# Moving router steps, layer norm and a quarter of the grouped scaling in a two-layer transformer kernel

## The reference, cut to what matters

```python
xn = layernorm(x)
x = x + L0_attn(xn) + L0_ffn(xn)
# L0_attn: 16 query heads of 64 over 4 key/value heads, rotary, causal with a decaying bias:
scores = Q @ K.T / 8 + polarity_bias + (1 - gtp) * NEG
out = softmax(scores) @ V @ Wo
# L0_ffn: y = xn + mha(rmsnorm(xn, g1)), 16 heads of 16, rotary, causal; then y + moe(rmsnorm(y, g2)):
probs = softmax(xf @ w_router)           # 8 experts
g, eidx = top_k(probs, 2)                # each expert then takes its 320 best tokens
```

## Time and profile before

| | us |
|---|---|
| median of 3 runs | 4479.95 |
| runs | 4475.49 to 4479.95 |
| profiled execution, own time | 4474.58 |
| its span | 4472.5 |
| TensorE busy | 3949.0 (88%) |
| DVE busy | 2916.6 (65%) |
| GpSimd busy | 2591.0 (58%) |
| ScalarE busy | 2582.7 (58%) |

### The profile page before, as it was taken

One profiled execution on the slowest core, in us unless ns is written; L12 is line 12 of the kernel. 1 busy time (PEld: TensorE's weight loads), 2 busy tenths in 40 slices (PEclk: granted clock), 3 DMA queues, 4 the chain that ended last, 5 costly groups with the idle time before them and its releaser, 6 DMA issues. The chain is left out here.

```text
span 4472.5 us, 105750 instructions
## 1 busy us (share of the span) xinstructions
PE 3949.0 (88%) x37596; PEld 2580.4 (58%) x37596; DVE 2916.6 (65%) x8580; ACT 2582.7 (58%) x6209; POOL 2591.0 (58%) x4110
## 2 busy tenths in 40 slices
PE   2899899999999999999999999829499999999999
PEld 1555555555555555555555556526266666666666
DVE  3665666665666656656666656562377777878786
ACT  2556556566565565565565665502166767777776
POOL 2567577586585675675765865625354545555452
PEclk7999999999999999999999999959799999999999
DMA  4334234243243233342432432123333343434341
GB/s 109 69 74 91 65 93 84 60 103 73 72 89 73 72 86 73 85 91 60 98 77 67 95 75 73 48 92 59 48 52 59 49 62 49 62 50 60 56 54 24
DMA packets 215158, 317.07 MB, mean 71 GB/s; under 512 B 22192, under 2 KB 161776, under 8 KB 212592
## 3 DMA queue, kind: packets, MB, share of 16 engines
q1 hardware_dynamic: 209520, 300.88, 32.8%
q0 software_dynamic: 3968, 5.25, 0.7%
q10 hardware_dynamic: 1152, 4.19, 0.2%
HBM read 126.66 MB, written 32.59 MB: 36 GB/s over the span
## 5 line engine op out<-in xcount | busy, mean ns | idle before, releaser
L1380 POOL TENSOR_SCALAR l_prob_wo<-l_prob_wo,l_recip_g 128x128 f32<-128x128 f32 (+3 forms) x1024 | 1097.8, 1089 | 232.3 <-DVE l_recip_g L966 231.7
L1820 DVE TENSOR_REDUCE l_neg_max<-l_bank 128x1 f32<-128x512 f32 x1024 | 681.0, 684 | 288.0 <-PE l_bank L1659 287.0
L1946 ACT ACTIVATE l_pts<-l_bank 128x512 f32<-128x512 f32 x1024 | 593.4, 597 | 310.1 <-PE l_bank L1674 301.4
L960 DVE CUSTOM_DVE_ANT_0 l_prob_wo<-l_bank,l_bias 128x128 f32<-128x128 f32 (+3 forms) x1024 | 477.1, 485 | 412.4 <-PE l_bank L683 388.5
L1219 ACT ACTIVATE l_prob_wo<-l_prob_wo,l_neg_max_g 128x128 f32<-128x128 f32 (+3 forms) x1024 | 571.0, 559 | 294.4 <-DVE l_neg_max_g L960 291.3
L947 DVE CUSTOM_DVE_ANT_0 l_bank<-l_bank,l_mask 128x128 f32<-128x128 f32 (+3 forms) x1024 | 502.9, 499 | 354.8 <-PE l_bank L632 347.1
L1211 ACT ACTIVATE l_pts<-l_bank 128x128 f32<-128x128 f32 (+3 forms) x1024 | 438.4, 437 | 451.3 <-PE l_bank L650 435.2
L694 PE MATMUL l_bank<-ident,l_prob_wo 128*128 128x128 f32 x2560 | 432.7, 283 | 95.4 <-POOL l_prob_wo L1380 43.4
L694 PEld LDWEIGHTS l_bank<-ident,l_prob_wo 128*128 128x128 f32 x2560 | 287.9, 141 | 335.8 <-POOL l_prob_wo L1380 191.5
L1659 PE MATMUL l_bank<-next_ks,l_qs 96*128 96x512 bf16 x1024 | 394.9, 386 | 60.0 <-DMA next_ks<-l_parts 30.5
L1368 POOL CAST l_max_parts<-l_neg_max 128x4 bf16<-128x4 f32 x256 | 49.9, 195 | 631.1 <-DVE l_neg_max L947 630.8
(11 more groups left out here) (261 smaller groups left out, 8083.7 us busy)
## 6 DMA issues: line engine op xcount, KB each, us to landing
l_bias<-bias SPq DMA_DIRECT2D x128, 512.0 KB, 4.4
l_qs<-l_parts SPq DMA_DIRECT2D x384, 128.0 KB
l_ks<-l_parts SPq DMA_DIRECT2D x192, 128.0 KB
next_ks<-l_parts SPq DMA_DIRECT2D x192, 128.0 KB
l_x<-in_x SPq DMA_DIRECT2D x32, 512.0 KB, 4.6
l_kT<-l_bias SPq DMA_DIRECT2D x128, 128.0 KB, 3.3
l_qT<-l_arena SPq DMA_DIRECT2D x128, 128.0 KB, 3.3
l_qT<-l_bias SPq DMA_DIRECT2D x128, 128.0 KB, 3.0
```

Source lines behind the costliest of these rows:

```text
L960: nc.vector.tensor_tensor_reduce(prob[qt][:, i, :], G4[v % 4][:, 0:w], bias[:, g % 2, i, T - w:T], -1.0 / ROOT, 3.0e38, ALU.add, ALU.min, ...
L1380: nc.gpsimd.tensor_scalar(prob[qt][:, i, :], prob[qt][:, i, :], recip_g[:, k:k + 1], None, ALU.mult).then_inc(s.g_scaled, 1)
L1820: nc.vector.tensor_reduce(neg_max[:, n % (2 * UNITS):n % (2 * UNITS) + 1], S[n % SB][:, :], AX.X, ALU.max, negate=True).then_inc(s.max_rea ...
L1946: nc.scalar.activation(pts[:, q % 2, u % H, :, :], TB[u % 2][:, :].rearrange("p (j q) -> p j q", j=NT), ACT.Exp, scale=DS ** -0.5).then_in ...
```

## The change

- Router: step 0 stays in slot 119; the rest becomes six steps, in slots 24, 26, 32, 37, 41 and 48 of the next frame. The gate transpose moves from slot 20 to 52, its copy from 21 to 53, its store on SP behind the first two bias loads.
- Layer norm of batch c + 1 (not c): statistics in slots 114 to 117, variance in 120, centring in 123 to 126 of frame f, the power on GpSimd in 121. Batch 0 is normed in the first slot of frame -1. The squares move on ScalarE from slots 12 to 15 to slots 2 to 5. The x load moves on SP behind the bias load of group 7, ahead of the store of the normed batch; for batch 1 behind the stacking of batch 0.
- GpSimd: each pair of rotations, rests and lows is spread over two slots, most a slot or two apart.
- Scaling: for pairs with qt 0 and 1, unit i = 1 is scaled on DVE, right behind the pair's reciprocal. That is 16 of 64 per frame.

```diff
+        def scaled_on_pool(p, i):
+            return i == 0 or p % NT > 1
+
+        def scaled(b, p, i):
+            qt = p % NT
+            if scaled_on_pool(p, i):
+                return s.g_scaled, 6 * (PAIRS * b + p // NT) + (1, 2, 3, 5)[qt] + i
+            return s.g_scaled_v, 2 * (PAIRS * b + p // NT) + qt + 1
...
-                    pe.wait_ge(s.g_scaled, v + 1)
+                    pe.wait_ge(*scaled(b, p, i))
...
-                        if r == 20:
+                        if r == 52:
                             fill_gT(f - 1, 1)
...
                     nc.vector.reciprocal(recip_g[:, k:k + 2], sums_g[:, k:k + 2]).then_inc(s.g_recip, 1)
+                    if not scaled_on_pool(p, 1):
+                        dve.wait_ge(s.g_recip, BEATS * b + p + 1)
+                        v = prob[p % NT][:, 1, :]
+                        nc.vector.tensor_scalar(v, v, recip_g[:, k + 1:k + 2], None, ALU.mult).then_inc(s.g_scaled_v, 1)
...
-                        if r == 21:
+                        if r in (24, 26, 32, 37, 41, 48):
+                            router(f - 1, 1 + (24, 26, 32, 37, 41, 48).index(r))
+                        if r == 53:
                             copy_gT(f - 1)
...
-                        if r in (119, 122, 124, 126):
-                            router(f, (119, 122, 124, 126).index(r))
+                        if r == 119:
+                            router(f, 0)
                     if there(c):
-                        if 2 <= r < 6:
-                            statistics(c, r - 2)
-                        if r == 7:
-                            variance(c)
-                        if 10 <= r < 14:
-                            centre(c, r - 10)
...
+                    if c == 0 and r == 0:
+                        for t in range(NT):
+                            statistics(0, t)
+                        variance(0)
+                        for t in range(NT):
+                            centre(0, t)
+                    if there(c + 1):
+                        if 114 <= r < 118:
+                            statistics(c + 1, r - 114)
+                        if r == 120:
+                            variance(c + 1)
+                        if 123 <= r < 127:
+                            centre(c + 1, r - 123)
                     if n == -1:
                         make_bias()
...
-                        if 12 <= r < 16:
-                            squares(c, r - 12)
+                        if 2 <= r < 6:
+                            squares(c, r - 2)
...
                         if r >= 68:
-                            scale(f, (r - 68) // 2, r % 2)
-                        if r in (7, 12, 17):
-                            rotate_g(f, (r - 7) // 5)
+                            if scaled_on_pool((r - 68) // 2, r % 2):
+                                scale(f, (r - 68) // 2, r % 2)
+                        if r in (6, 8, 12, 13, 17, 18):
+                            rotate_g(f, (6, 8, 12, 13, 17, 18).index(r) // 2, (6, 8, 12, 13, 17, 18).index(r) % 2)
...
-                        if r == 87:
-                            rotate_g(f, 4)
+                        if r in (87, 89):
+                            rotate_g(f, 4, (r - 87) // 2)
...
-                        if r == 68:
-                            rotate(c, 1)
-                        if r == 73:
-                            rest(c, 1)
-                        if r == 78:
-                            low(c, 1)
+                        if r in (66, 67):
+                            rotate(c, 1, r - 66)
+                        if r in (73, 74):
+                            rest(c, 1, r - 73)
+                        if r in (78, 80):
+                            low(c, 1, (r - 78) // 2)
...
+                sp.dma_start(x[:, :, :], a["x"][0]).then_inc(s.x_loaded, 16)
                 for f in range(-1, B + 1):
                     c = f + 1
-                    if there(c):
-                        wait(sp, s.xp_ready, 2 * f)
-                        if f > 0:
-                            sp.wait_ge(s.xp_ready, 2 * f)
-                        sp.dma_start(x[:, :, :], a["x"][c]).then_inc(s.x_loaded, 16)
...
                     if there(f):
                         load_bias(f, 7)
+                    if there(f) and there(c + 1):
+                        sp.wait_ge(s.xp_ready, 2 * (f + 1))
+                        sp.dma_start(x[:, :, :], a["x"][c + 1]).then_inc(s.x_loaded, 16)
+                    if f == -1:
+                        sp.wait_ge(s.ln, LN_STEPS)
+                        sp.dma_start(x[:, :, :], a["x"][1]).then_inc(s.x_loaded, 16)
+                    if there(f):
                         sp.wait_ge(s.xf_ready, NT * (f + 1))
```

More of the change, by code:

```diff
@@ L539, in layer0 @@
             sem(n) for n in ("scores_ready", "max_ready", "split", "max_turned", "max_placed", "t_ready", "exp_ready", "pv_ready", "out_turned"))
-        s.g_scores, s.g_max, s.g_exp, s.g_recip, s.g_scaled, s.g_turned, s.g_copied_v, s.g_copied_a, s.g_pv, s.g_out = (
-            sem("g_" + n) for n in ("scores", "max", "exp", "recip", "scaled", "turned", "copied_v", "copied_a", "pv", "out"))
+        s.g_scores, s.g_max, s.g_exp, s.g_recip, s.g_scaled, s.g_scaled_v, s.g_turned, s.g_copied_v, s.g_copied_a, s.g_pv, s.g_out = (
+            sem("g_" + n) for n in ("scores", "max", "exp", "recip", "scaled", "scaled_v", "turned", "copied_v", "copied_a", "pv", "out"))
         s.w_ready = sem("w_ready")
@@ L1087, in router @@
                         link(nc.vector.tensor_tensor(pr[:, :, :], pr[:, :, :], scalars[:, 1, :].unsqueeze(2).to_broadcast([P, NT, E]), ALU.mult))
+                    if step == 2:
                         for t in range(NT):
@@ L1090, in router @@
                         link(m)
-                    if step == 2:
+                    if step == 3:
                         for t in range(NT):
@@ L1095, in router @@
                         link(nc.vector.tensor_copy(top_f[:, :, :], top_i[:, :, :]))
+                    if step == 4:
                         for t in range(NT):
@@ L1098, in router @@
                         link(m)
-                    if step == 3:
+                    if step == 5:
                         for t in range(NT):
@@ L1102, in router @@
                         link(m)
+                    if step == 6:
                         link(nc.vector.tensor_tensor(one_hot[:, :, :], pr[:, :, :], lg[:, :, :], ALU.mult))
@@ L1380, in scale, with rotate_g @@
                     nc.gpsimd.tensor_scalar(prob[qt][:, i, :], prob[qt][:, i, :], recip_g[:, k:k + 1], None, ALU.mult).then_inc(s.g_scaled, 1)
-                def rotate_g(b, m):
+                def rotate_g(b, m, half):
                     w = work[(1, 0, 1, 1, 0)[m]]
@@ L1385, in rotate_g, with rotate, rest, low @@
                         pool.wait_ge(*W.emptied(("rope", b, m, e)))
[L1386 to L1389 removed]
+                    nc.gpsimd.tensor_tensor(w[:, half, :], w[:, half, :], w[:, 2 + half, :], (ALU.subtract, ALU.add)[half]).then_inc(s.turned_g, 1)
+                def rotate(c, a2, half):
                     for e in range(2):
                         pool.wait_ge(*W.emptied(("qk", c, 2 * a2 + e)))
[L1392 to L1403 removed]
+                    nc.gpsimd.tensor_tensor(arena[:, half, :], arena[:, half, :], arena[:, 2 + half, :], (ALU.subtract, ALU.add)[half]).then_inc(s.rot_ready, 1)
+                def rest(c, a2, e):
+                    pool.wait_ge(s.high_done, 4 * c + 2 * a2 + e + 1)
+                    nc.gpsimd.tensor_tensor(arena[:, 2 + e, :], arena[:, e, :], parts[2 * a2 + e][:, 0, :], ALU.subtract).then_inc(s.rest_ready, 1)
+                def low(c, a2, e):
+                    pool.wait_ge(s.mid_done, 4 * c + 2 * a2 + e + 1)
+                    nc.gpsimd.tensor_tensor(parts[2 * a2 + e][:, 2, :], arena[:, 2 + e, :], parts[2 * a2 + e][:, 1, :], ALU.subtract).then_inc(s.low_done, 1)
                 def scale_out(b, g):
@@ L1423, in _ @@
                     c = f + 1
+                    if c == 0 and r == 0:
+                        power(0)
+                    if there(c + 1) and r == 121:
+                        power(c + 1)
                     if there(f):
@@ L1452, in _ @@
                             nc.gpsimd.tensor_tensor(rms[:, :], mean_sq[:, :], minus_half[:, :], ALU.pow).then_inc(s.pow_rms, 1)
[L1453 to L1464 removed]
+                        if r in (40, 41):
+                            rotate(c, 0, r - 40)
+                        if r in (49, 50):
+                            rest(c, 0, r - 49)
+                        if r in (54, 56):
+                            low(c, 0, (r - 54) // 2)
+                        if r in (66, 67):
[4 more added lines that the diff above has]
+                            low(c, 1, (r - 78) // 2)
             @block.sync
@@ L1517, in _ @@
                         sp.dma_start(x[:, :, :], a["x"][f]).then_inc(s.x_again, 16)
-                    if there(f - 1):
```

(2 more changed lines are left out.)

39 lines of the change are left out of this document (11 added, 28 removed).

## The result

The changed kernel takes 4452.9 us in the median (4451.8 to 4455.8, 5 runs) against 4479.95 for the kernel before (4475.5 to 4485.5, 5 runs): ratio 0.994, interval 0.9925 to 0.9954. It is faster by 27 us. The forecast was 4498, slower; the time lies at the very end of its range, and the sign is wrong.

What follows compares the result with a forecast made beforehand. TensorE, busy 88% of the span, was taken as the bound. Frame terms -24.0 (15 frames) and +30.1 (14 frames), plus +17.4 at the start, gave +23.5 on 4474.6: 4498 us, range 4452 to 4535.

Steps and rivals of the forecast that it cites:

- Start: Start of layer 0: bias tables and first row maximum wait for batch 1's x load and layer norm, +17.4 us.
- The x load: Slot 114: DVE stalls 3.2 us for the next batch's x, making TensorE late by 1.8 us per frame.
- Router in slots 24 to 48: nothing: The router's six pieces hide in DVE's waits for scores there: no cost, or 0.5 us per frame if uncovered.
- -0.15: Slot 124: the router's 1.4 us leaves, but centring and a scaling take its place, -0.15 us per frame.
- Last slots otherwise, +0.35: Last slots besides the x wait: variance in slot 120 +0.5, router's leaving -0.15, together +0.35 us per frame.
- DVE's share of the scaling, +1.0: Grouped half: DVE's scalings delay five of eight copies for transposes by 0.2 us each, +1.0 us per frame.
- GpSimd, -1.2: Grouped half: sixteen scalings leave GpSimd and TensorE's waits on it shrink, -1.2 us per frame.
- the 0.68 us at 1259.78: A TensorE wait on GpSimd, to vanish with half a pair and a scaling less before it.
- Small-head half, -1.4: Slot 17: GpSimd's earlier first rotation lets key halves land sooner, shortening TensorE's wait by 1.4 us per frame.
- Faster: Rival: all 2.65 us of waits on GpSimd go, x stall hidden, DVE's scaling costs 0.2; 4439 us, chance 0.16.
- third rival: Slower by much: DVE's scalings wait out GpSimd's running one, 48 us more, 4546 us; chance 0.08.

Runs made afterwards that it cites:

- Experiment 2: The changed kernel with the x load of the next batch issued on SP ahead of the bias load of group 7: 4420.7 us, ratio 0.9876.
- Experiment 11: The changed kernel with GpSimd's pairs in one piece again: 4493.1 us, ratio 1.0016 to the kernel before.

## Why the prediction was wrong

The sum was 23.5, the profiles differ by -20.7: 44 us. Of these frames 0 to 14 hold 33, frame 15 and the experts' stage 8.5, chance in layer 1 7.4, and the start -4.6 (it was worse than I said). By part, with the ratios above times 4480:

| part | booked in the prediction | put in alone | put back |
|---|---|---|---|
| layer norm's move | +17.4 + 25.2 + 7.0 and a share of -21 | +89 | -66 |
| router's move | 0, and a share of -0.15 x 14 | -48 | +42 |
| pairs spread | -18 and a share of -21 | -22 | +34 |
| quarter on DVE | +15 | -25 | +15 |

Put in alone, the four make -6, together -27: the parts help each other, and the layer norm's move most, at +89 alone and +66 beside the others. The clock is a large part of that: alone, the move adds eight frames with a lowered clock in slots 17 to 21 (1.7 us each) and seven in the last slots (1.0 each), and in the changed kernel there is none in either place. By these counts that is an estimated 20 of the 23 us; against the second profile of the kernel before, which has four and nine such frames, it is 15.

- **Start: right in mechanism, sized low.** 22.0 us against 17.4. x landed at 95.2, not 90.5; the layer norm (4.45) and the tables (29.6) took what the sum said.
- **The x load: right.** The wait is 3.9 us (46.4/12) instead of 3.2, and TensorE's loss 1.9 against 1.8. Experiment 2 shows it.
- **"Router in slots 24 to 48: nothing" and "-0.15": the step that failed by most.** That the pieces are hidden in their new place was right. What they cost in the old one was not asked. I had the row with 1.57 us on the table, and let the centring take the router's place, which kept the wait in the sum. The router's leaving is worth 2.5 to 2.8 us per frame, some 0.5 of it by the clock that is not lowered behind the wait.
- **"Last slots otherwise, +0.35": right only as a net sum.** It hides -2.5 for the router and +2.4 for the layer norm, which I had at +0.5 for the variance alone; GpSimd's power behind that variance, ahead of four scalings, was left out. Where only one of the two happens, the net no longer holds: in frames 14 and 15 no next batch is normed, so the router's share, the small-head half's 2.0 and the grouped half's 1.1 stand uncompensated. They make 5.6 us, and frame 15 was in fact 5.8 us shorter up to its last store, but frame 14 only 3.1, with 3.4 us more at the lower clock in its middle. Single frames differ by up to 2.5 us between two profiles of one kernel, so the match in frame 15 is partly luck. The sum counted 15 frames at -1.6 and left the sixteenth out.
- **"DVE's share of the scaling, +1.0" beside "GpSimd, -1.2": the sum of the two is what the steady frame had most wrong.** Five of the eight copies were to be late by 0.2 us; in the changed kernel TensorE is late for them in two slots, by 0.2 and 0.4, as much of the scaling falls in DVE's wait for the transpose ahead of the copy, which the earlier trace rows showed at 0.33 us. The relief of GpSimd outweighs that: the 0.68 us at 1259.78 went, as forecast, and came back as 0.79 when the scalings did. Together the grouped half gained 1.1 per frame, not 0.2.
- **The net of a steady frame.** It was missed by 0.9 us in the grouped half, 0.6 in the small-head half and 0.55 in the last slots, where the router's error of 2.4 hides behind the layer norm's of 1.9. Over 14 or 15 frames these make some 30 of the 33 us, so the router's term alone does not explain the wrong sign.
- **Small-head half, -1.4: right in mechanism, sized low.** 2.0 us. Experiment 11 puts the wait back into slot 17 (0.51 to 2.04 us) with the pairs, which fits the chain through GpSimd's first rotation that the prediction named; that rotation alone was not tested. The layer norm's leaving brings little without the split rotations: 0.4 us alone, and the lowered clock behind the longer wait turns it into a loss of 0.8.
- **The rivals.** "Faster" gave 4439 by another way, with GpSimd's waits gone and x in time. Neither came: the stall stood at 3.9 us and the waits on GpSimd fell by a tenth. The result had the sign of this rival and not its mechanism.
- **The 4546 of the third rival** did not come, but DVE scalings that wait out an operation of GpSimd exist; see below.

What stays open: why the wait in slot 17 is longer with the layer norm gone and the pairs whole (2.0 us and more) than in the kernel before (1.4 to 2.1) was not traced DMA by DMA, nor why the same wait lowers the clock in one frame and not in the next.

## What to carry to other kernels

When a step is moved, price its old place as carefully as its new one: find the wait of the bound engine behind it, and ask what is gone if it goes. Two moves into and out of the same slots must be priced one by one, not as a net sum, because frames at the edges and later edits see only one of them. Put parts of a change on the chip one by one, each alone and each taken out: here three of four parts gain and the fourth costs 62 us, and the whole hides it. And count a wait of the bound engine together with the clock of the work behind it, which can change from frame to frame at the same wait.

## What the hardware showed

**The clock behind a wait.** Waits of 1.57 and 0.25 us in a busy stretch were followed by 3.4 us at 1.2 GHz in seven of 14 frames of the kernel before, and 16 products then took 3.1 to 3.25 instead of 1.74 us; the other seven frames had the same waits and kept 2.4 GHz. Behind 0.44 us of waiting (router alone) or 0.86 (the changed kernel) in that slot the clock never fell. In all these kernels the longer wait in slot 63 (31.5 us in 13 frames, 2.4 each) has 3.4 to 6.8 us at the lower clock around or behind it in every one of frames 1 to 14. And the dips in the last slots go with the wait there: none in 14 frames in the kernels with the router moved and the wait in slot 126 below 1 us, seven to fourteen where it is 1.57 us and more. No experiment here removes the wait in slot 63.

**GpSimd and DVE.** In the changed kernel a scaling on DVE that starts while GpSimd runs one of its operations of two inputs with 256 or 512 elements per partition lasts until that one has ended: 45 of 45 such cases, ending 83 to 150 ns after it in the mean of each of the three lines. Beside a scaling on GpSimd, of one input, it ends when it will: of 99 cases that start during one, the 31 of 128x256 take 352 to 355 ns; of the 68 of 128x128 about half take 285 to 330 ns, most of the others 387 to 441, and the longest 687. Another 15 start during GpSimd's power (two inputs, 4 elements): one ends at its own speed, and 14 begin within 20 ns of the next 128x512 scaling on GpSimd and take 0.77 us, which no run here explains. Frame 6 has both (GpSimd, DVE; GpSimd, DVE):

```profile
1247.86 2.51 POOL L1416 TENSOR_TENSOR l_arena<-l_arena 128x512 f32<-128x512 f32 x2 [7.04 <-DVE l_arena L1025]
...
1248.17 1.05 DVE L979 TENSOR_SCALAR l_prob_wo<-l_prob_wo,l_recip_g 128x128 f32<-128x128 f32 x1
...
1269.90 2.14 POOL L1405 TENSOR_SCALAR l_prob_wo<-l_prob_wo,l_recip_g 128x512 f32<-128x512 f32 x2
...
1270.47 0.29 DVE L979 TENSOR_SCALAR l_prob_wo<-l_prob_wo,l_recip_g 128x128 f32<-128x128 f32 x1
```

The first two-input operation (of the two in that row) ends at 1249.13, the DVE scaling at 1249.22. The Trainium skill, SBUF — State Buffer, "Who interferes with whom", has whoever issues first hold the shared port pair for its whole instruction, and counts DVE's `tensor_scalar` among the instructions that can use that pair. The trace agrees beside the three lines of two-input operations and not beside the 99 scalings. In the prediction I had weighed the rule against a scaling on GpSimd only the earlier trace rows, which is the case in which it does not show. The price stayed small, as each of the 45 delays is at most 0.77 us (1.05 less 0.29) and DVE had idle time there.
